# Weight quantization spread over earlier stages, and hidden-activation quantization in batches of eight chunks, in a two-layer transformer on 8 cores

## The reference

```python
x = x + L0_attn(layernorm(x))
x = x + einsum('bsi,oi->bso', layernorm(x), sign(weight))   # layer 0 ffn
x = x + L1_attn_and_mlp(layernorm(x))
x = x + fp4_ffn(layernorm(x))                               # layer 1 ffn

def fp4_quant_dequant(x):       # blocks of 16 along the last dim
    scale = max(|xb|) / 6, at least 1e-12
    q = GRID[searchsorted(MID, |xb / scale|)] * sign(xb) * scale
def fp4_linear(x, w): return q(x) @ q(w).T
gate, y = fp4_linear(x, w_gate), fp4_linear(x, w_up)        # 1024 -> 2816
out = fp4_linear(silu(gate) * y, w_down)                    # 2816 -> 1024
```

## Time and profile before

| | us |
|---|---|
| median of 3 runs | 21343.29 (21202.61 to 21628.6) |
| the profiled execution | 21343.29 |
| its span, core 1 (slowest) | 21341.7 |
| spans of the 8 cores | 21141.6 to 21341.7 |
| TensorE busy on core 1 | 11588.5 (54%) |
| VectorE busy on core 1 | 8502.4 (40%) |
| ScalarE busy on core 1 | 2918.4 (14%) |

### The profile page before, as it was taken

One profiled execution on the slowest core, in us unless ns is written; L12 is line 12 of the kernel. 1 busy time (PEld: TensorE's weight loads), 2 busy tenths in 40 slices (PEclk: granted clock), 3 DMA queues, 4 the chain that ended last, 5 costly groups with the idle time before them and its releaser, 6 DMA issues.

```text
span 21341.7 us, 170472 instructions; the slowest of 8 cores (21141.6 to 21341.7 us)
## 1 busy us (share of the span) xinstructions
PE 11588.5 (54%) x52144; PEld 4708.3 (22%) x52144; DVE 8502.4 (40%) x11980; ACT 2918.4 (14%) x3627; POOL 1100.6 (5%) x2080
## 2 busy tenths in 40 slices
PE   4875598788843214554477761677710044444355
PEld 1322222222311001121111110466610011212122
DVE  4211267766131223113366642211177743343433
ACT  0000044444010000000033320100011111011111
POOL 0111000000001002110100000000000000000000
PEclk6776677877766657666677775889955566767677
DMA  2110101110223221001100013344411110101011
GB/s 71 45 34 19 39 6 31 31 30 12 99 87 99 78 65 44 26 19 49 57 24 25 24 48 131 117 145 142 145 51 47 39 40 27 53 32 47 32 48 50
DMA packets 522810, 1179.51 MB, mean 55 GB/s; under 512 B 71616, under 2 KB 227648, under 8 KB 508992
## 3 DMA queue, kind: packets, MB, share of 16 engines
q1 hardware_dynamic: 420928, 873.81, 12.8%
q0 software_dynamic: 100992, 294.78, 3.8%
HBM read 873.66 MB, written 269.48 MB: 54 GB/s over the span
## 4 chain that ended last, share of the span: by engine, by line
PE 42%; DVE 29%; DMA 13%; issue 8%; ACT 5%; DVEq 1%; POOL 1%; SPq 0%; ACTq 0%; POOLq 0%
PE PB L294 40%; DVE A L262 13%; DVE A L274 6%; ACT A L283 4%; DVE A L287 4%; DVE A L269 2%; DMA vst<-A 2%; PE PB L303 2%; DMA A<-w1hl_s 2%; DVE PB L274 1%; DVEq L56 1%; DMA n1st<-A 1%; DMA A<-A 1%; DMA y2own<-A 1%; DMA A<-w_s 1%
## 5 line engine op out<-in xcount | busy, mean ns | idle before, releaser
L294 PE MATMUL PB<-A 128*128 128x512 bf16 (+5 forms) x48320 | 10013.3, 442 | 3817.5 <-DVE A L262 2036.0
L294 PEld LDWEIGHTS PB<-A 128*128 128x128 bf16 (+2 forms) x48320 | 4202.0, 113 | 9533.0 <-issue 8255.4
L262 DVE TENSOR_TENSOR A<-A 128x1024 f32<-128x1024 f32 (+6 forms) x4388 | 4150.8, 946 | 2453.8 <-ACT A L283 1344.6
L303 PE MATMUL PB<-sb_iden,A 128*128 128x128 f32 x2000 | 662.2, 401 | 4603.2 <-DVE A L262 3645.8
L283 ACT ACTIVATE A<-PB 128x1024 f32<-128x1024 f32 (+3 forms) x1976 | 1863.8, 943 | 5725.6 <-DVE PB L262 2809.1
L283 ACT ACTIVATE A<-A 128x512 f32<-128x512 f32 (+5 forms) x1136 | 653.2, 575 | 7878.6 <-DMA A<-y2own 2669.5
L303 PEld LDWEIGHTS PB<-sb_iden,A 128*128 128x128 f32 x2000 | 338.9, 181 | 4981.0 <-issue 4980.8
L274 DVE SCALAR_TENSOR_TENSOR A<-A 128x512 f32<-128x512 f32 (+5 forms) x1376 | 1167.4, 848 | 146.0 <-DVE A L269 2.3
L294 PE MATMUL PB<-A,sb_ones 128*1 128x512 f32 x1280 | 699.6, 687 | 945.0 <-DMA w2hl_s<-A 510.0
L287 DVE COPY A<-PB 128x128 f32<-128x128 f32 (+1 forms) x1136 | 388.9, 342 | 1912.6 <-DMA vst<-A 1014.9
L287 DVE CAST A<-A 128x512 bf16<-128x512 f32 (+3 forms) x904 | 418.2, 463 | 1653.5 <-ACT A L283 751.2
(11 more groups left out here) (44 smaller groups left out, 2048.3 us busy)
## 6 DMA issues: line engine op xcount, KB each, us to landing
A<-w1hl_s SPq DMA_DIRECT2D x256, 512.0 KB, 3.9
A<-w2hl_s SPq DMA_DIRECT2D x64, 2048.0 KB, 8.6
A<-x_fm SPq DMA_DIRECT2D x192, 256.0 KB, 2.6
A<-y1st SPq DMA_DIRECT2D x192, 256.0 KB, 2.7
vst<-A POOLq DMA_DIRECT2D x512, 64.0 KB, 1.8
A<-y2st SPq DMA_DIRECT2D x128, 256.0 KB, 2.9
A<-y2own SPq DMA_DIRECT2D x128, 256.0 KB, 3.0
A<-A POOLq DMA_DIRECT2D x384, 64.0 KB, 1.9
```

The lines of the kernel that those rows point to most:

```text
L262: e.tensor_tensor(out=o, in0=a, in1=b, op=p), sem)
L294: return e.matmul(**kw)
L303: e.transpose(out=o, in_=i, identity=sb_iden[:]), sem)
```

## The change

1. **The weights' quantization moves.** `quant_weight` and its stage go. After L0's output projection (behind L771) `build_qw_steps` makes a list of 68 x 4 = 272 closures: for each slice of at most 1024 columns a load, a quantization, and two groups of up to 4 transposes with split and two stores. `tick(n)` runs the next n of them, that is, it puts their instructions into the engines' queues at that place. It is called once per token tile in `ln_stats`, and with 2 after each chunk of LN1, each output of W0 and each iteration of the select loop: 8 x 17 = 136 steps (34 slices) in LN1, 128 (32 slices) in W0, and the last 8 (2 slices) in the first four iterations of select.
2. **`quantize_slice`** scales in place (`a` instead of a buffer of its own), which saves one scratch buffer; the instructions are otherwise the same.
3. **LN1** is interleaved: statistics of one token tile, then the normalization of its 8 chunks, with `M1`/`R1` of 512 columns instead of 4096, and one barrier ahead of the first tile.
4. **`g_stage` becomes `gh_stage`.** The 22 hidden chunks go in groups of 8, 8 and 6. The transposed activations of a group are collected in `HTM` (4 token groups x 2816). After a group, each of the 4 token groups is quantized in one slice of 1024 (or 768) columns, and its 8 (or 6) blocks are transposed back and split.
5. `XQb` becomes a single buffer, `HTM` lies over `XTM`, and `xb` serves both `x_stage` and `d_stage`; `x_stage` starts with a wait for TensorE and for the stores.

```diff
+        def mk_load(src, si, w):
+                g.wait("sync", sem)
+                lt = st["lastten"].get(si % 2)
+                if lt is not None:
+                    g.wait("sync", TEN, lt)
+                st[("ldv", si % 2)] = g.dma("sync", natb_w[si % 2][:, 0:w], src, sem)
+        def mk_quant(si, w):
+                g.wait("vector", sem, v)
+                g.wait("scalar", sem, v)
+                st[("qv", si)] = quantize(natb_w[si % 2][:, 0:w], w,
+                                          natb_w[si % 2][:, 0:w])
+        def mk_group(si, dst, oc, k0g, kloc, kn):
+                gp = st["gi"][0] % 2
+                st["gi"][0] += 1
+                pb = PB[2 + gp][:][:, 512:1024]
+                g.wait("tensor", VEC, st[("qv", si)])
+                for k in range(kn):
+                    tv = transpose(pb[:, 128 * k:128 * k + 128],
+                                   natb_w[si % 2][:, 128 * (kloc + k):
+                                                  128 * (kloc + k) + 128], sem=TEN)
+                g.wait("vector", TEN, tv)
+                sv_ = st["store"].get(gp)
+                if sv_ is not None:
+                    g.wait("vector", ssem, sv_)
+                split_hl(trv[:, 0:128 * kn], trv[:, 128 * kn:256 * kn],
+                         pb[:, 0:128 * kn])
+                g.dma("gpsimd", dst[0][oc, :, k0g:k0g + kn, :]
+                      .rearrange("p k c -> p (k c)"), trv[:, 0:128 * kn], ssem)
+                g.dma("gpsimd", dst[1][oc, :, k0g:k0g + kn, :]
+                      .rearrange("p k c -> p (k c)"), trv[:, 128 * kn:256 * kn], ssem)
...
     for t in range(NT):
+        ln_stats(lambda fc, t_, t=t: rd3.rd(y1st[fc, :, 512 * t:512 * t + 512],
+                                            "tensor", "scalar"),
+                 1, M1, R1, sqb, barrier=(t == 0))
         for fc in range(FC):
             ch = rd4.rd(y1st[fc, :, 512 * t:512 * t + 512], "vector")
...
             split_hl(ZNh[:, c], ZNl[:, c], ztmp)
+            tick(2)
...
-    quant_weight(wg_nat, DIC, D, wgq_s)
-    quant_weight(wu_nat, DIC, D, wuq_s, barrier=False)
-    quant_weight(wd_nat, FC, DI, wdq_s, barrier=False)
...
-        def g_stage(t):
-            for oc in range(DIC):
+        def gh_stage(t):
+            for g0 in range(0, DIC, 8):
+                gn = min(8, DIC - g0)
+                for oc in range(g0, g0 + gn):
...
                     for i in range(4):
                         tv2 = transpose(tp_slot(i), ub[:, 128 * i:128 * i + 128], sem=TEN)
                         g.wait("vector", TEN, tv2)
-                        vcopy(ht[:, 128 * i:128 * i + 128], tp_slot(i), sem=VEC)
-                qv = quantize(ht, 512, ht, xv=VEC.v)
-                g.wait("tensor", VEC, qv)
-                for i in range(4):
-                    tv3 = transpose(tp_slot(i), ht[:, 128 * i:128 * i + 128], sem=TEN)
-                    split_hl(HQH[:, cc], HQL[:, cc], tp_slot(i))
+                        vcopy(HTM[:, DI * i + 128 * oc:DI * i + 128 * oc + 128],
+                              tp_slot(i), sem=VEC)
+                for i in range(4):
+                    hs = slice(DI * i + 128 * g0, DI * i + 128 * (g0 + gn))
+                    qv = quantize(HTM[:, hs], 128 * gn, HTM[:, hs], xv=VEC.v)
+                    g.wait("tensor", VEC, qv)
+                    for kc in range(g0, g0 + gn):
+                        tv = transpose(tp_slot(kc),
+                                       HTM[:, DI * i + 128 * kc:DI * i + 128 * kc + 128],
+                                       sem=TEN)
+                        g.wait("vector", TEN, tv)
+                        split_hl(HQH[:, cc], HQL[:, cc], tp_slot(kc))
```

More of the change, by code:

```diff
@@ L334, in rd, with quantize_slice @@
             return b
+    qsl_state = [None]
+    QSCR = {}
+    def quantize_slice(X, Fcols, out, xv=None):
+        nb = Fcols // 16
+        assert Fcols <= 1024
+        a = QSCR["A"][:, 0:Fcols]
+        s1 = QSCR["S1"][:, 0:Fcols]
+        s2 = QSCR["S2"][:, 0:Fcols]
+        gsn = QSCR["G"][:, 0:Fcols]
+        m = QSCR["M"][:, 0:nb]
+        ss = QSCR["SS"][:, 0:nb]
+        r = QSCR["R"][:, 0:nb]
+        if qsl_state[0] is None:
+            g.wait("scalar", VEC)
+        else:
+            g.wait("scalar", VEC, qsl_state[0])
+        if xv is not None:
+            g.wait("scalar", VEC, xv)
+        act(a, X, AF.Abs)
+        act(gsn, X, AF.Sign, sem=SCA)
+        g.wait("vector", SCA)
+        g.op("vector", lambda e, o=m, i=a: e.tensor_reduce(
+            out=o, in_=i.rearrange("p (b k) -> p b k", k=16), axis=AX.X, op=ALU.max))
+        ts(ss, m, C6_1, ALU.mult)
+        stt(ss, m, C6_2, ss, ALU.mult, ALU.add)
+        ts(ss, ss, float(f32(1e-12)), ALU.max, sem=VEC)
+        g.wait("scalar", VEC)
+        act(r, ss, AF.Ln)
+        act(r, r, AF.Exp, scale=f32(-1.0), sem=SCA)
+        g.wait("vector", SCA)
+        rbc = r.unsqueeze(-1).broadcast_to((128, nb, 16))
+        sbc = ss.unsqueeze(-1).broadcast_to((128, nb, 16))
+        a3d = a.rearrange("p (b k) -> p b k", k=16)
+        tt(a3d, a3d, rbc, ALU.mult)
+        ts(s1, a, 0.25, ALU.is_gt)
+        stt(s1, a, 0.75, s1, ALU.is_gt, ALU.add)
+        stt(s1, a, 1.25, s1, ALU.is_gt, ALU.add)
+        stt(s1, a, 1.75, s1, ALU.is_gt, ALU.add)
+        ts(s2, a, 2.5, ALU.is_gt)
+        stt(s2, a, 3.5, s2, ALU.is_gt, ALU.add)
+        stt(s2, a, 5.0, s2, ALU.is_gt, ALU.add)
+        stt(s2, a, 5.0, s2, ALU.is_gt, ALU.add)
+        stt(s2, s1, 0.5, s2, ALU.mult, ALU.add)
+        tt(s2.rearrange("p (b k) -> p b k", k=16),
+           s2.rearrange("p (b k) -> p b k", k=16), sbc, ALU.mult)
+        tt(out, s2, gsn, ALU.mult, sem=VEC)
+        qsl_state[0] = VEC.v
+        return VEC.v
@@ L336, in build_program, with quantize, tick @@
+    def quantize(X, Fcols, out, xv=None):
+        v = None
+        o = 0
+        while o < Fcols:
+            w = min(1024, Fcols - o)
+            v = quantize_slice(X[:, o:o + w], w, out[:, o:o + w], xv=xv)
+            o += w
+        return v
+    qw_steps = []
+    def tick(n=1):
+        for _ in range(n):
+            if qw_steps:
+                qw_steps.pop(0)()
     g.dma("sync", sb_vecs[:], vecs, LDQ)
@@ L774, in build_program @@
+    build_qw_steps()
     if stop_phase <= 4:
@@ L1452, in x_stage @@
                 c = slice(512 * t, 512 * t + 512)
-                if xb_ten[0] is not None:
-                    g.wait("vector", TEN, xb_ten[0])
+                g.wait("vector", TEN)
                 tt(xb, ch, M4[:, c], ALU.subtract)
@@ L1591, in d_stage @@
                 g.wait("vector", STQ)
[L1592 removed]
+                tt(xb, pv, ch, ALU.add, sem=VEC)
                 pg_guard[2 + oc % 2] = VEC.v
                 g.wait("gpsimd", VEC)
[L1595 removed]
+                g.dma("gpsimd", y_out[oc, :, 512 * t:512 * t + 512], xb, STQ)
         x_stage(0)
         for t in range(NTO):
[L1599 removed]
+            g_end = gh_stage(t)
             if t + 1 < NTO:
```

220 lines of the change are left out of this document (132 added, 88 removed).

## The result

The changed kernel takes **0.9642 of the time of before (95%: 0.9580 to 0.9704), 3.6% less**. Medians over 12 runs each: 21444.19 us before (21202.61 to 21714.26), 20915.40 after (20517.77 to 21043.05). The ratio compares executions without a die that ran longer at a lower granted clock; 8 of after's 12, the profiled one among them (0.695 on cores 0 to 3, 0.705 on the others), had one, so the medians alone lie only 2.5% apart. For the FFN I therefore read the cores one by one, and rest sizes on several kernels.

A forecast was written before the change was run, and what follows sets the result against it. No engine bounds the whole, so each stage was read by itself: 21343 - 259 (quantization moved) - 424 (gh_stage) = 20660, plus 70 for the slowest core's clock: 20,730 us, range 20,450 to 21,020.

The forecast's parts named there:

- Part 1: Weight quantization moved into LN1, W0 and select: 755 + 542 + 31 = 1328 us come back against 1587, -259 us.
- Part 2: gh_stage, the FFN's hidden chunks quantized by group: 659 us per token tile against 765, -424 us.
- the 70 of the correction: Added for the slowest core: denser TensorE work at a granted clock of about 0.81, 165 us, part there today.
- The W0 step: W0, 32 slices: TensorE's queue order sets a period of 26.7 us; W0 becomes 863 us, +542.
- The 37: W0: us for loading the weights, from 321 - 284, added to 826 to give 863.
- Rival (c): Moved quantization gains nothing: loads, ScalarE's table or statistics wait in line, 3.8 us more per slice; 20,990; chance 0.14.
- rival (d): Slower: VectorE waits in each group for the previous group's stores on GpSimd's queue; +940, 21,670; 0.04 with other losses.
- rival (e): W0 set by VectorE alone, period 23.2 us, 110 less: 20,620; chance 0.22 shared with rival (b).
- One sign in my list: Profile after: LN1 and W0 both with VectorE busy over 80%.
- the 12.0 us of matmuls: FFN hidden chunk: 48 matmuls taken at 12.0 us within a 15.5 us chunk; 10.3 if the clock stays at 1.00.
- Rival (b): FFN: clock does not fall over the 3.5 us gap, 150 us less: 20,580; chance 0.22 shared with rival (e).
- Rival (a): Lower clock spreads: g chunks and d stages at 0.81 on every core, +165 and 99 us; 20,920; chance 0.18.

The follow-up runs named there:

- lag: The changed kernel with each weight slice's two transpose groups queued one slice later, behind the next slice's quantization; 0.9546 of the time of before.
- p2_only: The kernel before with only the new FFN (grouped quantization of the hidden activation), weights still quantized in their own stage; 0.9800 of the time of before.
- w0_only: The changed kernel with weight slices interleaved only in W0 (32); the other 36 run bare behind the own-token normalization; 0.9626 of the time of before.
- fwd_pipe: The changed kernel with each hidden chunk's transposes and copies put behind the next chunk's matmuls; 0.9547 of the time of before.

## Why the prediction was right, step by step

The predicted 20,730 is 0.971 of 21343; 0.9642 of 21343 is 20,580, inside the range, and faster than I had it. The median in microseconds (20,915) is inside too. The sum was 150 us too slow, by three terms that all erred the same way: 25 us in Part 1, some 50 in Part 2 and the 70 of the correction.

**Part 1.** Averaged over the cores, LN1 rose by 743 us (755 predicted), W0 by 519 (542; on core 1 from 321 to 863, as forecast), select by 31.5 (31), and 1578 went: -284 instead of -259. The W0 step held in its mechanism as well: periods set by TensorE's order, and `lag` took away what the order cost. That core 1 came out at 863 to the microsecond is luck: a period of a slice of 1024 is 26.2 on average and not 26.7, and from the stage's first transfer (6954.9) to its first reduce (7002.8) there are 48 us and not 37. The 37 was badly founded, as 321 less the 269 of the outputs is 52, and the 284 that I subtracted comes from no row. In LN1 the sum held while two terms were off: the slice costs 22.5 and not 22.2, and the interleaving gives 20 us that I had at nothing. Rival (c) is dead, since the moved part came back with 1294 us, 34 less than the 1328 of the sum and not 260 more; rival (d) too, since the list of waits has no store of weights; rival (e) is what `lag` is and after is not. One sign in my list was wrong: VectorE was to be busy over 80% of LN1 and W0, and it is 70% in both (816.67 of 1165, 601.70 of 863). I counted the queue as held and forgot that busy time leaves out its waits: 140 us for the statistics, 64 for Ln and Exp, 53 for transposes, and 144 for outputs.

**Part 2.** The gap of 3.5 us, the removed table loads (6 a stage) and a slice of 27.5 hold: the four slices behind a group in `p2_only`, core 0, last from the first Abs at 17618.68 to the end of the last split at 17730.19, 111.5 us, where the sum gives 110 and a table load of 1.28. The mis-sized term is the 12.0 us of matmuls. It was to be 10.3 or 12.0, and I took one end; it was each of them about half of the time, and 11.34 on average over the 88 groups of core 0. 88 x 0.65 is 57, and 424 + 57 = 481 against the 470 to 481 of `p2_only`. Rival (b) was thus half true. I had read the earlier trace rows as "mostly it falls"; there only the length of the gap was like the new one, 24 matmuls stood behind it instead of 48, and the new gap has four transposes in it.

The Trainium skill, "ScalarE: Activation LUTs", "What ACT_TABLE_LOAD costs", has 1283 ns for the load, which the row of after shows too, and about 1380 ns more for a drain. By that, Part 2 would have gained 210 us more than by my sum; it gained about 50 more, and the chunk's matmuls account for them. The trace speaks against the drain here.

**The correction of 70 us** is the step that failed. The cores of lower clock were 184 us behind in the FFN before (4412 - 4228) and are 173 behind in `p2_only` (3931 - 3758). I had written that part of the 165 us is there today; all of it was. These cores already lost time in the chunks of before: 13.5 us a group of 48 on core 3 against 12.07 on core 0. Without the 70 the sum is 20,660, and with the measured -284 and -475 it is 21343 - 759 = 20,584, 0.9644. The ratio is 0.9642; that they agree so closely is luck, as its interval is 0.6% to either side and the untouched stages alone vary by more.

**Rival (a)**, the lower clock on every core, did not come: in every kernel of this study at least four cores ran the FFN mostly at the full level.

## What to carry to other kernels

Work moved into another stage gains only where it takes turns with an engine that was idle *at that point of the queue*: 34 slices in LN1, where VectorE was the engine that counted, cost what they cost bare; 32 in W0 gained some 200 us and would have gained 95 more with one step of distance between the quantization and its transposes. Before tuning the work between two matmul groups, see whether the groups can be issued one step ahead; here the three reorderings of the FFN (222 + 588 + 222 us) were worth more than both parts of the change (284 + 475). And when steps are dealt out by count, count again after reordering them: one slice changed its stage unseen.

## What the hardware showed that I had not expected

**In the FFN one pair of cores of each die is the slower one, not the whole die.** Two cores of one die in the same stretch of the kernel before, both in a d stage with TensorE busy for nearly all of 100 us:

```profile
core 0: us, PE busy (x) PEld busy (x) DVE busy (x) ACT busy (x) POOL busy (x), PEclk, DMA share, GB/s
20240.00:20340.00 100.00, 98.60 (x457) 44.50 (x456) 4.84 (x7) 0.00 (x0) 3.78 (x7) 1.00 0.40 129
...
core 2: us, PE busy (x) PEld busy (x) DVE busy (x) ACT busy (x) POOL busy (x), PEclk, DMA share, GB/s
20240.00:20340.00 100.00, 99.38 (x376) 41.41 (x381) 4.15 (x6) 0.00 (x0) 3.23 (x6) 0.81 0.37 117
```

The granted clock is 1.00 on one and 0.81 on the other (each core's time counts from its own first instruction). In all ten profiled executions exactly one pair of each die (0,1 or 2,3; 4,5 or 6,7) was the slower one in the FFN; in before it was 2,3 and 4,5, in after 0,1 and 6,7. It is a tendency and no fixed state: core 4 of before had a d(2) at 1.00, core 3 of after a d(0) at 0.81, and in `w0_only` the pairs of the second die lie only 13 us apart at their closest cores. The pair that is slow in the FFN was mostly the quicker one in layer 0's projections (2382 to 2395 us from the start to the first store of attention, against 2542 to 2566, in before), so that the spans of the cores nearly even out. The Trainium skill, "TensorE: Matmul & The Clock Gate", Part 1, describes a limiter of 13/16 for the whole die; the value agrees with the rows (0.81 on core 2), the reach doesn't (1.00 on core 0 of the same die). What picks the pair I have not settled.

**The clock over a gap of 3.5 us is not one or the other.** The same gap with the same transposes in it was followed by 48 matmuls in 10.52 us 41 of 76 times on one core, and in 11.4 to 13.2 us the other 35, mostly 12.2; without it (`fwd_pipe`, 64 groups) it was always 10.52.
